# Four of a batch's eight normalised rows of t moved from ScalarE to GpSimd, with the steps behind them moved by a bank or two

## What is computed

```
x = x + layernorm(mixers(layernorm(x)))          # t, the stream after the first half
x = x + layernorm(expert(layernorm(x)))          # u = layernorm(t) feeds the expert
mixers: 4 mixers, each  h_s = a_s*h_{s-1} + sigmoid(g)*tanh(v)  along the sequence,
        g, v, a from three 256x256 products; the best 2 of 4 per token, weighted
expert: 1 of 8 per batch, picked from the mean of u over the sequence (z);
        y = relu(u W_down + b) W_up + b, times the expert's probability
```

## Time and profile before

| | |
|---|---|
| median of 3 runs | 698.22 us (697.70 to 699.17) |
| profiled execution, own time | 698.33 us |
| its span, first to last instruction | 696.5 us |
| busy: PE, DVE, ACT, POOL | 626.3 (90%), 596.4 (86%), 445.0 (64%), 160.1 (23%) us |
| mean granted TensorE clock | 0.966 |
| PE stands for | `normed` 22.8 us in 8 waits, one of 16.8 at the end; `z_wr` 8.3 us in 8 waits |

### The profile page before, as it was taken

The page is one execution under the profiler, slowest core; times in us unless marked ns, Lnnn a source line. Parts: engine busy times, 40 slices in busy tenths (PEclk is TensorE's granted clock), DMA queues, the critical chain, the costliest instruction groups (busy, mean ns, idle before and its releaser), DMA issues. The chain is left out here.

```text
span 696.5 us, 11112 instructions
## 1 busy us (share of the span) xinstructions
PE 626.3 (90%) x3457; PEld 329.8 (47%) x3457; DVE 596.4 (86%) x1304; ACT 445.0 (64%) x785; POOL 160.1 (23%) x238
## 2 busy tenths in 40 slices
PE   3999989999999999899999999899999999999032
PEld 2445444555445554455445554455545554554021
DVE  7593999889997899889998899889998889788966
ACT  2848638774678548774678548775678546777033
POOL 2006043003710072003710072003710042001101
PEclk9999999999999999999999999999999999999655
DMA  8700531120332031120332031120340010000003
GB/s 229 198 1 0 121 122 32 31 73 1 122 61 72 1 125 31 32 73 1 121 61 72 1 124 32 32 73 1 121 61 12 1 62 1 1 11 1 0 16 116
DMA packets 63712, 39.16 MB, mean 56 GB/s; under 512 B 34934, under 2 KB 63642, under 8 KB 63642
## 3 DMA queue, kind: packets, MB, share of 16 engines
q1 hardware_dynamic: 63644, 38.34, 20.3%
HBM read 21.03 MB, written 8.39 MB: 42 GB/s over the span
## 5 line engine op out<-in xcount | busy, mean ns | idle before, releaser
L1219 PE MATMUL ps_main<-x_feat,w_hi 128*128 128x512 f16 x1536 | 471.2, 381 | 2.4 <-ACT x_feat L539 1.5
L1219 PE MATMUL ps_main<-x_feat,w_lo 128*128 128x512 f16 x768 | 292.5, 381 | 0.0
L1219 PEld LDWEIGHTS ps_main<-x_feat,w_hi 128*128 128x128 f16 x1536 | 150.6, 98 | 179.7 <-issue 2.2
L836 DVE TENSOR_TENSOR_SCAN hid<-decay_s,value_s 128x1024 f32<-128x1024 f32 (+1 forms) x64 | 144.6, 2260 | 6.7 <-DVE value_s L856 1.7
L560 ACT ACTIVATE value_s<-ps_main,vecs 128x512 f32<-128x512 f32 x128 | 88.6, 692 | 84.1 <-PE ps_main L1219 84.1
L560 ACT ACTIVATE decay_s<-ps_main,vecs 128x512 f32<-128x512 f32 x128 | 88.5, 691 | 62.0 <-PE ps_main L1219 47.7
L1219 PEld LDWEIGHTS ps_main<-x_feat,w_lo 128*128 128x128 f16 x768 | 75.3, 98 | 83.9 <-issue 1.1
L560 ACT ACTIVATE gate_s<-ps_main,vecs 128x512 f32<-128x512 f32 x128 | 88.7, 693 | 39.2 <-PE ps_main L1219 34.3
L445 POOL TENSOR_TENSOR root_y<-root_in_y,neg_half 128x8 f32<-128x8 f32 (+1 forms) x9 | 18.8, 2091 | 311.1 <-DVE root_in_y L946 311.1
L849 DVE SCALAR_TENSOR_TENSOR mixed<-ps_aux,comb,mixed 128x256 f32<-128x256 f32 x192 | 77.2, 474 | 12.0 <-PE ps_aux L1229 9.7
L856 DVE TENSOR_TENSOR value_s<-gate_s,value_s 128x1024 f32<-128x1024 f32 (+1 forms) x66 | 78.2, 1185 | 5.6 <-ACT value_s L560 5.0
(11 more groups left out here) (159 smaller groups left out, 557.6 us busy)
## 6 DMA issues: line engine op xcount, KB each, us to landing
x_in<-in_L_attn_x SPq DMA_DIRECT2D x16, 512.0 KB, 4.3
resid<-in_L_attn_x SPq DMA_DIRECT2D x7, 1024.0 KB, 5.2
out<-resid SPq DMA_DIRECT2D x7, 1024.0 KB, 4.5
expert<-experts SPq DMA_DIRECT2D x8, 192.5 KB, 2.2
w_stage<-in_L_attn_Wg SPq DMA_DIRECT2D x4, 256.0 KB, 4.0
w_stage<-in_L_attn_Wd SPq DMA_DIRECT2D x4, 256.0 KB, 5.3
w_stage<-in_L_attn_Wv SPq DMA_DIRECT2D x4, 256.0 KB, 5.6
u_split<-in_L_ffn_W_down SPq DMA_DIRECT2D x4, 256.0 KB
```

The costliest lines, as they stand in the source:

```text
L836: dve.tensor_tensor_scan(states(pc), staged(decay_s, pc, pc.c), staged(value_s, pc, pc.c), start, ALU.mult, ALU.add).then_inc(scanned, 1)
L1219: ins = pe.matmul(ps_main[:, i % BANKS], w[:, 3 * m + kind, k, half * P:(half + 1) * P], feat(low, bt, k, c), start=(n == 0), stop=(n == 3 ...
```

## The change

1. **GpSimd writes half of `normed`.** ACT keeps tiles 0, 1 (before bank 20) and 4, 5 (before bank 21). POOL writes tiles 2, 3 and then 6, 7, each pair with a `u_rest`, when `t_scaled` has come. The eighth batch's own rows stay as they were.
2. **u turned and copied earlier.** `turn_u` stands before banks 23 and 24 (was 23 and 25), `high_u` too (was 24 and 25). `turn_u` waits for `u_ready` and `u_rest`.
3. **z in front of the low parts.** DVE runs `route_in` ahead of `low_u`. PE's `route` is before bank 27 (was 28), and `turn_h(bt, 0)` before bank 29 (was 28, behind `route`).
4. **`start_mix` one bank later**, before banks 30 to 33.
5. **`low_h` in halves**: copy and subtraction of 512 columns twice instead of 1024 once.

The first piece is POOL's, the third to fifth are ACT's, the last two PE's:

```diff
+            def normalise_t(pv):
+
+                pool.wait_ge(t_scaled, done(pv))
+                pool.sem_inc(rest_begun, 1)
+                for c in range(C):
+                    for t in pool_tiles(c):
+                        ins = pool.tensor_scalar(normed[:, t], resid[:, pv.par, t], mul_by["t"][:, t:t + 1],
+                                                 shift["t"][:, t:t + 1], ALU.mult, ALU.add)
+                    ins.then_inc(u_rest, 1)
...
                     power("t", t_root_in, t_root, pv)
+                    normalise_t(pv)
                     power("y", y_root_in, y_root, pv)
...
-                NORM_X, MIX = (7, 29) if pv else (29, 25)
+                NORM_X, MIX = (7, 30) if pv else (29, 25)
...
-                        if 20 <= i < 24:
-                            normalise_t(pv, pair(i, 20))
-                        if i in (24, 25):
-                            high_u(pv, i - 24)
+                        if i in (20, 21):
+                            normalise_t(pv, scalar_tiles(i - 20))
+                        if i in (23, 24):
+                            high_u(pv, i - 23)
...
                 rank_mixers(bt)
+                route_in(pv)
                 low_u(pv)
                 weights_of(bt)
-                route_in(pv)
                 route_logits(pv)
...
-                low_h(pv)
+                for c in range(C):
+                    low_h(pv, c)
...
                     pe.wait_ge(u_ready, done(pv, c))
+                    if not pv.cut:
+                        pe.wait_ge(u_rest, done(pv, c))
...
-                        if i in (23, 25):
-                            c = (i - 23) // 2
+                        if i in (23, 24):
+                            c = i - 23
                             pe.wait_ge(combined, summed_up(pv, 3, c))
                             turn_u(pv, c)
-                        if i == 28:
+                        if i == 27:
                             route(pv)
+                        if i == 29:
                             for c in range(C):
                                 low_u_done(pv, c)
                                 turn_h(bt, 0, c)
```

More of the change, by code:

```diff
@@ L190, in mixer_kernel @@
             sem("t_root_in"), sem("t_root"), sem("t_scaled"), sem("u_ready"), sem("u_turned"))
+        rest_begun, u_rest = sem("rest_begun"), sem("u_rest")
         x_factor, t_factor = sem("x_factor"), sem("t_factor")
@@ L269, in state_tile, with scalar_tiles, pool_tiles @@
             return hid[:, (KT * m + k) % 4, t * P:(t + 1) * P]
+        def scalar_tiles(c):
+            return tiles(c)[:T // C // 2]
+        def pool_tiles(c):
+            return tiles(c)[T // C // 2:]
         y_rows = x_in[:, 0]
@@ L592, in normalise @@
             def normalise(key, rows, scaled, ready, b, ts):
+                act.wait_ge(scaled, done(b, ts[0] // (T // C)) if b.cut else done(b))
                 for t in ts:
-                    act.wait_ge(scaled, done(b, t // (T // C)) if b.cut else done(b))
                     ins = act.activation(normed[:, t], rows[:, t], ACT.Identity, bias=shift[key][:, t:t + 1],
                                          scale=mul_by[key][:, t:t + 1])
-                    if t % (T // C) == T // C - 1:
-                        ins.then_inc(ready, 1)
+                ins.then_inc(ready, 1)
             def normalise_x(nx, ts):
@@ L679, in last @@
                         router_sigmoids(pv)
-                    if 29 <= i < 33:
-                        start_mix(bt, pv, pair(i, 29))
+                    if 30 <= i < 34:
+                        start_mix(bt, pv, pair(i, 30))
                     if i == 34:
```

## The result

The changed kernel takes **730.47 us** (median of 4 runs, 728.40 to 730.95) against 698.14 before in the same comparison (4 runs, 697.70 to 699.17): a ratio of 1.0446, 95% interval 1.0431 to 1.0461. It is 32.3 us slower. The forecast was 709.4 with a range of 700 to 721, so the direction was right and the size was not.

The account below looks back on a forecast made before the run. PE was taken as nearly full, its lost time between the shift of t and `down`, with DVE the loop's other half. Six stages at +1.68 (+10.1) and a seventh at +1.1 gave +11.2 on 698.33: 709.4 us, range 700 to 721.

Parts of the forecast that it names:

- So I take one tile for each end of a DVE instruction: Behind the shift of t: one GpSimd tile gets through at each end of a two-input DVE instruction.
- `split_x` and L856 overlap their predecessor by 0.08, so there a tile should cost 0.09 + 0.08 + 0.10 = 0.27: Overlapping DVE instructions behind the shift: a GpSimd tile entering there costs DVE 0.27 us, bounds 0.10 and 0.48.
- the first term of the sum, -0.07: PE's first turn, the transposes ahead of bank 23: starts at 362.49 against 362.56, 0.07 us sooner a stage.
- Rival B: No GpSimd tile enters where DVE's instructions overlap; first turn 3.27 late, stage +3.34, total +21, 719.4 us; chance 0.22.
- +1.68 at the second turn: Second turn, one bank sooner: PE arrives at 364.69, waits for GpSimd's tile 7, starts at 366.37; +1.68 us a stage.
- `route`, -1.07: PE's `route` matmul: with z computed first, its wait of 1.07 us a stage is hidden behind products 24 to 26.
- `start_mix`, +1.29: `start_mix` at bank 30: `down` waits 1.53 for ACT's pairs where it waited 0.24, +1.29 us a stage.
- `low_h` in halves, -0.15: `low_h` split in two: `combine` can start sooner, room between 0 and 0.37, taken as -0.15 us a stage.
- The seventh stage, +1.1: Stage without `split_x`: tile 2 behind L856, tile 3 behind the scan; first turn +1.00, stage sum +1.1 us.
- Rival C: GpSimd's tiles behind the shift: each holds DVE for its whole 0.48; +2.6 us a stage, 715.6 us; chance 0.10.
- D: Rival: GpSimd is not held by DVE, both turns start on arrival, stage -0.7, 693.5 us; chance 0.12.
- E: Rival: `down` waits no more than before because ACT catches up; 700.5 us; chance 0.11.

Follow-up runs that it names:

- experiment 2: Changed kernel with DVE waiting on its own semaphore between the halves of `split_x` and behind the second: 711.37 us against 699.41, ratio 1.0173.
- experiment 3: Changed kernel with one wait of DVE on its own semaphore, behind the second half of `split_x` only: 713.55 us against 699.26, ratio 1.0207.
- experiment 5: Changed kernel with 18 more matmuls, results unused, in PE's wait before the first turn in six stages: 718.73 us against 699.12, ratio 1.0280.
- Experiment 1: Kernel before with only GpSimd's half of `normed`, all other steps at their old banks: 725.08 us against 699.41, ratio 1.0371.
- experiment 7: Kernel before with `route` at 27, `turn_h` at 29, `low_h` in halves, no GpSimd tiles, `start_mix` at 29: 700.74 us against 699.12, ratio 1.0025.
- experiments 7 and 8: The second of these is the kernel of experiment 7 with `start_mix` at bank 30 instead of 29: 709.51 us, ratio 1.0150.
- experiment 4: Changed kernel with DVE waiting ahead of `split_x` until GpSimd has written its four tiles: 712.92 us against 699.41, ratio 1.0191.

## Why the prediction was wrong in size

**The step that failed: "So I take one tile for each end of a DVE instruction", and with it "`split_x` and L856 overlap their predecessor by 0.08, so there a tile should cost 0.09 + 0.08 + 0.10 = 0.27".** The row that this came from had a gap of 0.09 between DVE's instructions; it was carried to ends that overlap. There no tile gets in; it waits. Tile 2 waited for three DVE instructions instead of one, tile 3 for the scan, and the first term of the sum, -0.07, was +3.20. Experiments 2 and 3 show it by making such gaps: the first turn starts 6.34, 4.28 and 3.23 us behind the shift with none, one and two. Rival B had this mechanism, and its size to 0.07 (+3.27), with a chance of 0.22; its +21 stands against the 19.6 of experiment 5, where the clock is whole. For the case with overlap the prediction had no row, and it gave that case too small a chance. That the direction came out right is in part luck: the term that carried it, +1.68 at the second turn, did not come, and GpSimd's lateness showed at the first turn, where the sum had a small gain.

**A term that stood nowhere: the clock.** Neither the sum nor a rival asked what PE does behind a wait of 4 us. It works on at a granted 0.50 for about 3 us in one stage and 5.6 in the next: 12.7 us over the run (experiment 5), and 12.5 when the stages of the trace are added up. B's 719.4 with the 12.7 is 732, which is the result within 2. B itself was priced as if PE's time were the same before and behind a wait.

**Second turn, +1.68:** not there (B said so), since tiles 6 and 7 are done at 381.98, 3.2 before PE comes to them; in experiment 2, where the tiles came as forecast, it was 1.63.

**`route`, -1.07:** right, 1.9 left and that in the tail; but the credit is not z's alone. Experiment 1 shows that a late PE hardly waits there anyhow (3.3 in all, 1.9 of them in the tail, without z first), and experiment 7 that z first takes nothing away while u's second chunk is copied before bank 25.

**`start_mix`, +1.29:** right. 1.13 a stage by the trace, 1.25 by experiments 7 and 8.

**`low_h` in halves, -0.15:** -0.03 in the trace, which is too little to tell from nothing.

**The seventh stage, +1.1:** its two tiles went in behind L876 and behind the scan, as forecast, and its first turn starts 4.20 behind the end of the shift, against 3.05 before: +1.15 where the sum had +1.00.

**Rival C** (each tile holds DVE for 0.48) is wrong: `split_x` took 2.36 and L876 1.22 with a tile waiting, as before, and where a tile got in, the DVE instruction behind it took 0.16 to 0.25 more (experiment 2), or 0.07 (L877 of experiment 3). Its own terms, 6 x 2.6 + 1.1, give 714.9 and not 715.6. The Trainium skill, "SBUF — State Buffer", "Who interferes with whom", says that a DVE instruction with two SBUF inputs contends with a GpSimd instruction that reads SBUF; the trace agrees, a tile of 0.54 took 3.48 beside them. What the prediction quoted from there for C, that the other side blocks fully, the page says of DVE's 2-port modes; how much of that time is DVE standing still no record here shows. **D** is refuted by the same rows. **E** is refuted by the 1.37 at `down`.

## What to carry to other kernels

Price work that you move to GpSimd not by its own duration but by when DVE lets it in. Look what DVE runs in that window, how many SBUF inputs each instruction has, and whether the records show a gap between them (the gaps that let a tile in here were 0.03 to 0.13 us). If there is none, count the whole chain. If the piece is small and DVE's chain is what blocks it, let DVE write it: here DVE had the two tiles ready 0.76 us behind the shift, GpSimd 6.2. Where a change makes PE wait for microseconds in a full stretch, add what the granted clock does behind the wait. And moved steps that feed each other (u, z, `route`, `start_mix`) can be worth nothing one by one, so price each with the others where they were.

## What the runs showed of the hardware beyond that

- POOL is not held by every neighbour. In the changed kernel, eight tiles of x take 0.54 each, as long as the undisturbed tiles of experiment 4. Beside the first of them DVE runs an instruction with one tensor from PSUM and one from SBUF, beside the last one with a single tensor from SBUF. POOL and DVE:

```profile
352.94 4.32 POOL L493 TENSOR_SCALAR normed_x<-x_in,mul_by_x,shift_x 128x256 f32<-128x256 f32 x8 [0.22 <-POOL shift_x L486]
```

```profile
352.69 3.23 DVE L869 SCALAR_TENSOR_TENSOR mixed<-ps_aux,comb,mixed 128x256 f32<-128x256 f32 x8 [0.52 <-PE ps_aux L1251]
355.96 2.71 DVE L747 BATCH_NORM_STATS2 stats_a<-mixed 128x6 f32<-128x256 f32 x8
```

- A DVE instruction with two SBUF inputs that overlaps such a predecessor in the records by 0.08 us left GpSimd no way in; with a self-wait between them, seen as a gap of 0.03 or 0.12 us, one tile got in each time, and the kernel was faster for it (730.5 to 711.4). The overlap alone does not do it: the scan is overlapped by 0.07 by an instruction that reads PSUM (L824), and the waiting tile ended 0.36 behind the scan all the same.
- In an otherwise full PE the granted clock fell to 0.50 around the end of an idle stretch of 4.0 to 4.4 us in all six stages of the loop, and PE worked at it for about 3 us in one stage and 5.6 in the next, by turns. Around a wait of up to 2.5 us it fell in four of six stages (experiment 4), at one of 2.2 to 2.3 in three of five (experiment 3), and with waits of 1.1 to 1.6 (experiment 2) it stayed at 1.00. Why stages with the same wait differ stays open.
